# A decoder kernel on one core: self attention's first scores placed beside the last expert ticks, the last two norms cut into pieces, the last output flips issued one product ahead

## The reference

```python
def _L0_ffn_ref(...):                       # 2048 tokens, 8 expert bases, 2 shared blocks
    gate = (xt @ w_gate).reshape(T, K, I);  up = (xt @ w_up).reshape(T, K, I)
    basis = jax.nn.silu(gate) * up
    ...                                     # routing: 4 of 128 experts mix the 8 bases
    out = jnp.einsum('teh,te->th', down, coeff)
    shared = jax.nn.silu(xt @ shared_w_gate) * (xt @ shared_w_up) @ shared_w_down
    return (out + shared).reshape(B, S, H)

def _L1_attn_ref(x, Wq, Wk, Wv, memory, memory_norm, memory_weight):
    q = x @ Wq.T;  k = x @ Wk.T;  v = x @ Wv.T      # 4 x 8 query heads and 8 key heads of 16
    probs = jax.nn.softmax(einsum(qh, kh) * scale)
    a_dot = einsum(probs, vh)
    sigma_q = jax.nn.elu(q.reshape(b, s, N_QUERY, D_KV))
    a_mem = sigma_q @ memory / (sigma_q @ memory_norm)
    return a_dot * (1.0 - w) + a_mem * w            # w = sigmoid(memory_weight)

x = _layernorm(x + _L0_ffn_ref(x, ...))
x = _layernorm(x + _L1_attn_ref(x, ...))            # batch 8, 256 positions
```

## Time and profile before

| | before |
|---|---|
| median of three runs | 2317.35 us |
| the profiled execution, whole time | 2319.68 us |
| its span (first to last instruction) | 2317.8 us |
| mean granted clock of PE | 0.96 of full |
| PE busy | 2098.1 us (91%) |
| DVE busy | 1305.4 us (56%) |
| ACT busy | 1031.1 us (44%) |
| POOL busy | 892.2 us (38%) |
| chain that ended last: PE, DVE, ACT | 42%, 11%, 6% |

### The profile page before, as it was taken

The page is one execution under the profiler, slowest core; times in us unless marked ns, Lnnn a source line. Parts: engine busy times, 40 slices in busy tenths (PEclk is TensorE's granted clock), DMA queues, the critical chain, the costliest instruction groups (busy, mean ns, idle before and its releaser), DMA issues.

```text
span 2317.8 us, 37875 instructions
## 1 busy us (share of the span) xinstructions
PE 2098.1 (91%) x13663; PEld 1668.6 (72%) x13677; DVE 1305.4 (56%) x3359; ACT 1031.1 (44%) x2318; POOL 892.2 (38%) x944
## 2 busy tenths in 40 slices
PE   7799999899999987999999999988999868888877
PEld 6688888687777875887777788866565446676645
DVE  3454445654555455644537633356777756667767
ACT  3332333444434433445542222324666546677753
POOL 1753444334343322214433024634444335445302
PEclk9899999899999998999999999998999988999988
DMA  3402101111111111111101011123333410000001
GB/s 129 137 33 69 46 33 51 46 42 46 49 46 43 41 39 53 44 35 53 47 27 39 27 37 37 66 35 56 52 57 51 108 57 15 15 29 7 15 1 73
DMA packets 58312, 109.05 MB, mean 47 GB/s; under 512 B 7184, under 2 KB 35088, under 8 KB 54672
## 3 DMA queue, kind: packets, MB, share of 16 engines
q1 hardware_dynamic: 58128, 106.63, 15.8%
...
## 4 chain that ended last, share of the span: by engine, by line
PE 42%; DVE 11%; ACT 6%; issue 3%; POOL 1%; SPq 0%; DMA 0%; ACTq 0%; DVEq 0%; POOLq 0%
PE PS L1330 18%; ACT xP L2628 3%; PE PS L1838 3%; PE PS L1938 3%; PE PS L1346 2%; DVE st L200 2%; DVE aM L2086 2%; PE PS L1906 1%; DVE PS L2746 1%; PE PS L2487 1%; PE PS L993 1%; PE PS L1005 1%; PE PS L1926 1%; PE PS L2524 1%; PE PS L1893 1%
## 5 line engine op out<-in xcount | busy, mean ns | idle before, releaser
L1330 PE MATMUL PS<-WH,bXH 128*128 128x512 f32 x640 | 258.2, 403 | 0.0
L1330 PE MATMUL PS<-WL,bXH 128*128 128x512 f32 x640 | 250.2, 391 | 0.0
L1330 PE MATMUL PS<-WH,bXL 128*128 128x512 f32 x640 | 250.1, 391 | 0.0
L1511 DVE SCALAR_TENSOR_TENSOR s<-s,PS 128x256 f32<-128x256 f32 x160 | 67.3, 421 | 294.7 <-ACT s L1462 294.5
L2086 DVE TENSOR_REDUCE aM<-PS 128x4 f32<-128x1024 f32 x128 | 153.7, 1221 | 49.3 <-PE PS L1906 48.4
L1462 ACT ACTIVATE s<-PS 128x256 f32<-128x256 f32 x160 | 61.6, 386 | 261.9 <-PE PS L1330 261.2
L1632 POOL TENSOR_TENSOR WL<-sg,WH 128x512 fp32r<-128x512 f32 x80 | 102.0, 1310 | 184.3 <-ACT WH L1446 184.3
L421 PE MATMUL PS<-aXH,QKH 128*128 128x512 f32 x384 | 157.3, 410 | 16.0 <-ACT sq L634 7.9
L1627 POOL TENSOR_TENSOR mixed<-mixed,s 128x256 f32<-128x256 f32 x112 | 82.6, 741 | 225.5 <-DVE s L1528 225.4
L421 PE MATMUL PS<-aXH,QKL 128*128 128x512 f32 x384 | 152.6, 397 | 0.0
L421 PE MATMUL PS<-aXL,QKH 128*128 128x512 f32 x384 | 152.6, 397 | 0.0
...
## 6 DMA issues: line engine op xcount, KB each, us to landing
...
aqs<-aQH SPq DMA_DIRECT2D x64, 128.0 KB, 4.2
...
```

The lines of the kernel that those rows point to most:

```text
L1330: mm = e.matmul(PS[:, b, :], x[:, kc, c:c + 128], y[:, kc, :], start=kc == 0 and n == 0, stop=kc == KC - 1 and n == 2)
```

## The change

Five things are moved; the arithmetic stays as it is.

1. Self attention's slots start earlier beside the ticks. Slots -34 to -29 now stand behind ticks 141 to 146, ten slots go by twos behind ticks 147 to 151, one behind 152, four by twos behind 153 and 154, and slots -13 to -6, the first eight scores, behind ticks 155 to 162. `alone` is now slot -5.
2. `early` loses the wait for tick 151's product; it becomes a wait of its own (`weights_end`) at slot -17, and POOL's clearing of the first `aks` buffer moves from slot -28 to slot -17. SP still waits for both at slot -28.
3. Work around the first slots moves later: `value_turn`, `elu`, `memory` of j = 0, `elu` and `memory` of j = 1, all preparing steps of j = 2 by six slots, `query`, `elu`, `memory` of j = 3, and `gate` from slot -27 to -16.
4. Norm 2 keeps its four statistics at ticks 156 to 159, one each; its root comes at slots 3 and 4 and its four ACT operations at slots 5 to 8. Norm 3 has its statistics in slots 10 to 13, its root at 15 and 16 and its ACT operations at slots 17 to 20.
5. From tick 159 on the flip is issued ahead of the output product of the same tick.

```diff
@@ experts0 @@
-    for p in range(NP - 1):
+    for p in range(NP - 2):
         n = 79 + 80 * (p // 2) + 4 * (p % 2)
         norm_at.update({n: ("stats", p), n + 1: ("newton", p), n + 2: ("apply", p)})
+    norm_at.update({156 + i: ("tile", i) for i in range(4)})
...
@@ experts0, tensor (the same in banks and vector) @@
-            for v in out_at.get(tick, ()):
-                out(v)
+            if tick < 159:
+                for v in out_at.get(tick, ()):
+                    out(v)
             for v in flip_at.get(tick, ()):
                 flip(v)
+            if tick >= 159:
+                for v in out_at.get(tick, ()):
+                    out(v)
...
-    K.early = (*K.cross_ends, w_lo.upto(20), d_lo.upto(3), r_mm.upto(4), t_mm.upto(152))
+    K.early, K.weights_end = (*K.cross_ends, w_lo.upto(20), d_lo.upto(3), r_mm.upto(4)), t_mm.upto(152)
...
@@ attention1 @@
+    shift = {("value_turn", 0): 8, ("elu", 0): 15, ("memory", 0): 9, ("elu", 1): 12, ("memory", 1): 11, ("elu", 2): 6, ("memory", 2): 2,
+             ("query", 3): 4, ("elu", 3): 4, ("memory", 3): 2}
...
-            put(base - lead, 6, what, j, i)
+            put(base - lead + shift.get((what, j), 6 if j == 2 else 0), 6, what, j, i)
...
-    put(-27, 7, "gate", 0)
+    put(-16, 5, "gate", 0)
...
-    for i, what in enumerate(("late1", "late2", "late3", "late4")):
-        put(-17 + i, 7, what, 0)
+    for p in (0, 1):
+        for i in range(4):
+            if p:
+                put(10 + i, 7, "late_tile", p, i)
+            put(5 + 12 * p + i, 7, "late_apply", p, i)
+        put(3 + 12 * p, 7, "late_stats", p)
+        put(4 + 12 * p, 7, "late_root", p)
...
-    first, alone, last = min(at), -17, max(at) + 1
+    first, alone, last = min(at), -5, max(at) + 1
...
@@ attention1, gpsimd @@
-            if at_slot in (-28, alone):
-                for w in early if at_slot == -28 else ends:
-                    e.wait_ge(*w)
-                for y in (0,) if at_slot == -28 else (1, 2):
-                    clear(y)
+            for w in {-28: early, -17: (weights_end,), alone: ends}.get(at_slot, ()):
+                e.wait_ge(*w)
+            for y in {-17: (0,), alone: (1, 2)}.get(at_slot, ()):
+                clear(y)
...
@@ decoder @@
-        beside_a1 = K.self_alone - K.self_first
-        order += [(X, 163 - 76 - beside_a1)]
-        for _ in range(beside_a1):
-            order += [(X, 1), (4, 1)]
-        order += [(4, a1.ticks - beside_a1), (5, K.own_slots - K.first_slot)]
+        order += [(X, 163 - 76 - 22)]
+        for n in 6 * [1] + 5 * [2] + [1] + 2 * [2] + 8 * [1]:
+            order += [(X, 1), (4, n)]
+        order += [(4, a1.ticks - (K.self_alone - K.self_first)), (5, K.own_slots - K.first_slot)]
```

83 lines of the change are left out of this document (46 added, 37 removed).

## The result

The changed kernel is slower: 2336.44 us (median of 4 runs, 2334.41 to 2340.62) against 2317.43 us of the kernel before in the same session. The ratio is 1.0081, with a 95% interval of 1.0065 to 1.0097. The profiled execution took 2337.94 us with a span of 2336.2, so 18.4 us more of span than before (2317.8). The forecast was slower, but by 6.8 us.

What follows compares the result with a forecast made beforehand. PE (its work, idle gaps and clock) was taken as the bound. To the first turned product -6.3, then +2.5 slots 0 to 4, +1.1 memory, +8.5 clock, +1.0 norms: +6.8 us, 2324.2 us; range over the cases 2308 to 2333.

Steps and rivals of the forecast that it cites:

- Step 7: PE's clock: half speed after each of three long waits, costing 1.5, 3.5 and 3.5 us, +8.5; bounds 3 and 13.
- step 6: Slots 0 to 4: 11.8 us of PE work and a 2.7 us wait at slot 3; 14.5 against 12.0, +2.5.
- T0 to T5: Stretch from the first turned product (T0) to the sixth slot's score (T5): 14.5 us forecast against 12.0.
- The landing: Before the first score: the last query DMA lands after 4.4 us, bounds 2.6 and 5.2; PE waits 8.7 us.
- Rival C: Query DMAs land in 2.6 us instead of 4.4, three waits end 1.8 earlier: no change, 2319 us; chance 0.07.
- Step 1: At slot -28, PE waits 4.2 us for POOL before turning x, 2.1 more before `key`; bounds together 4 to 8.
- Step 3: Last ticks: 4.6 us each, then DVE sets the pace, 9.8 us to the last output's add (E), 11.8 later.
- Steps 4 and 5: Behind the last output: PE waits some 7 us for query DMAs, then 8.3 us; first turned product 6.3 earlier.
- Rival B: After the waits PE's clock returns at once, so the 8.5 us goes: no change, 2316 us; chance 0.17.
- Step 8: Slots 3 to 20: the norms' pieces on DVE and ACT are mostly covered, +1.0 us, between 0 and 9.3.
- rival D: Slots 3 to 20: the norms' pieces are not covered, +8.3 us more, 2332 us; chance 0.12.
- Rival A: Operands of slots -28 and -13 arrive in time: first turned product 21.3 us earlier, -13.2 in all, 2304 us; chance 0.16.

Runs made afterwards that it cites:

- split_on_dve: The changed kernel with the eleven low parts of self attention's weights made by DVE instead of POOL: 2337.23 us, ratio 1.0068 to the kernel before.
- kept_busy2: The changed kernel with unread PE products filling the waits before the first two keys and the scores of passes 0, 1 and 2: 2332.06 us, ratio 1.0060.
- before_turn: The kernel before with only the flip ahead of the output product from tick 159 on: 2318.29 us, ratio 1.0000.
- before_busy2: The kernel before with 24 unread PE products in the 5.39 us wait ahead of the first turned product: ratio 0.9995.
- all_three: The changed kernel with the memset two slots earlier, second-pass queries waiting for tile 159 alone, and low weight parts on DVE: 2315.43 us, ratio 0.9973.
- best2: The changed kernel with earlier memset, second-pass queries behind tile 159, slots three ticks later, third-pass queries and x turning earlier: 2304.58 us, ratio 0.9942.

## Why the prediction was wrong

**The direction and the mechanism were right.** Waits for feeds at the places named, each followed by a slow clock. The size was not: +18.4 against +6.8.

**Step 7 with step 6 failed, T0 to T5: +9.1 instead of +2.5.** Step 6 forecast the wait at slot 3 (2.7 us), but step 7 priced the clock behind "three such waits (steps 1, 2, 4)" and left this one out: its clock was put at nothing, without a reason. The wait was 4.20 us long and was followed by a slow stretch of 9.6 us, the longest of the four: 1.5 us more of wait, 4.7 of clock and 0.3 of small idle moments. The work, 11.8 us by step 6, was right (21.1 - 4.2 - 0.3 - 4.7 = 11.9; the items of step 6 add up to 11.6). This is 6.6 of the 11.6 us that were missing. The Trainium skill (TensorE: Matmul & The Clock Gate, HAM oscillation) has the price paid once for each long DMA wait; the trace agrees for the three that end with a DMA (9.74, 8.20 and 4.20 us), and I did not count the last. The kernel before had shown more than the one such price that I cited, too: 1562 to 1572 and 1590 to 1600.

**The landing was too short.** 4.4 us was taken, 5.5 to 5.7 measured from the last issue to PE's start, three times, above the upper bound of 5.2 as well. With the memset 4.3 us later than forecast (1532.6 instead of 1528.3) this makes the first score 1546.2 instead of 1540.7; the wait there was 9.74 instead of 8.7, since PE was late itself. Rival C's 2.6 us was further off still: a row of six such DMAs lands in 5.5. The Trainium skill (DMA: Bandwidth & Descriptors, Anatomy of one DMA) gives 2.0 us and the bytes at 436 GB/s for a DMA that GpSimd issues, 2.3 us for 128 KB; these are issued by SyncE, and no run here shows GpSimd's.

**Step 1 was right in its sum, wrong in its place.** 7.28 us instead of 6.3, all of it before the key, none before the turning, for the shared count that split_on_dve brought out. The weights landed 1.6 us later than I had it (ACT's first copy at 1482.33), as everything was 1.6 us later at M.

**Step 3 was nearly right.** The ticks took 5.0 us instead of 4.6. It is PE that paces them, not DVE: PE has no gap, at full clock (busy PE, PEld, DVE, ACT, POOL, then clock, DMA share, GB/s):

```profile
1551.00:1556.00 5.00, 5.00 (x25) 3.87 (x24) 3.74 (x6) 0.77 (x2) 0.73 (x1) 1.00 0.00 0
```

From tile 159's end at 1566.1 it was 9.1 us to E, where 9.8 was forecast (the items that step 3 lists for it add up to 10.4). **Steps 4 and 5:** the wait behind E was 8.20 instead of 7, and a further 1.69 for the low part of x was missed; E to T0 21.4 instead of 19.4.

**Step 7's three prices** were 2.1, 1.7 and 2.4 us, 6.2 instead of 8.5. The stretch they were taken from had been misread: 0.63 between 458 and 460 puts the clock's return at 459.5, not 458.5, and the price there at 3.9, not 3.4. So the prices came out below their model, not above. kept_busy2 shows that it is idleness that costs them. Rival B is out.

**Step 8's number was met, in part by luck.** +2.3 behind T5 where 2.1 was forecast (1.1 of it memory). But at slot 21's attended values the changed kernel is already 3.9 us behind (37.3 us from T5 against 33.4), with the wait of 2.07 and its slow clock in it, which the 1.0 us did not have. 1.5 of it comes back further on because the profile of the kernel before has a slow stretch there (1647 to 1651) that before_turn and before_busy2 don't have. So rival D holds in small: a wait of 2.07 to 2.15 us behind norm 3's root in every version with the two-part root, though in all_three with no slow clock behind it.

**The remaining 1.6 us** lie ahead of M, where PE's order was not changed. Measured at PE's end of tile 147, this place lies between 1491.4 and 1496.5 in the seventeen profiles of the table, so that a single profile can't be compared at the span's end to better than that. Rival A, the feeds in time, was worth what it promised once it was built: best2 is 13 us under the kernel before (0.0058 x 2317.4), as A's 13.2 had it, and by nearly the same sum. From M on its T0 is 21.0 us earlier (A: 21.3), T0 to T5 5.5 longer (A: 2.5, and 3.5 of clock) and the rest the same (A: 2.1 longer).
